# Attention in halves: value weights times g as f32r products of high and low parts, and raw expert weights in two places

## The reference

```python
h = h + attn(layernorm(h))   # q, k, v = x @ w_qkv, 16 heads of 64
                             # q = softmax(q * SCALE, axis=-1); k = softmax(k, axis=-2)
                             # context = q^T k over the tokens; out = context . v; out @ w_out + b_out
h = h + ffn(layernorm(h))    # sigmoid router, best 2 of 8 experts (4 of width 256, 4 of 512),
                             # relu(x @ w1)^2 @ w2, weighted by the two normalized probabilities
```

## Time and profile before

| | |
|---|---|
| median of 3 runs | 763.19 us (762.99 to 764.37) |
| the profiled execution | 760.92 us |
| its span | 759.1 us |
| TensorE matmul busy | 644.4 us (85%) |
| VectorE busy | 472.6 us (62%) |
| ScalarE busy | 304.7 us (40%) |
| GpSimd busy | 324.2 us (43%) |
| mean granted TensorE clock | 0.94 |

### The profile page before, as it was taken

How to read it: one execution, slowest core, us unless ns; L and a number is a source line. 1 busy time by engine, 2 the same in 40 slices (tenths; PEclk the granted TensorE clock), 3 DMA queues, 4 the chain that set the end, 5 groups by cost and what they waited for, 6 DMA issues and landing times. The chain is left out here.

```text
span 759.1 us, 15851 instructions
## 1 busy us (share of the span) xinstructions
PE 644.4 (85%) x5026; PEld 554.9 (73%) x5026; DVE 472.6 (62%) x1226; ACT 304.7 (40%) x664; POOL 324.2 (43%) x300
## 2 busy tenths in 40 slices
PE   6299677999999999999999998620999999988882
PEld 5299555788787877878878786510899999988772
DVE  2167566677987779777797775372645454555441
ACT  1324014445344353443534425302555555565551
POOL 6450134131370814608155170624144444466674
PEclk9699978999999999999999999955899999999997
DMA  7640288001110111101110020233244544467674
GB/s 235 206 92 2 56 214 306 3 1 56 44 70 2 57 56 55 59 8 69 39 57 29 11 75 1 82 116 108 60 80 72 86 81 78 81 102 116 106 116 49
DMA packets 38496, 59.44 MB, mean 78 GB/s; under 512 B 6110, under 2 KB 32218, under 8 KB 37786
## 3 DMA queue, kind: packets, MB, share of 16 engines
q1 hardware_dynamic: 23090, 35.76, 16.3%
q0 software_dynamic: 14496, 20.79, 15.0%
q10 hardware_dynamic: 808, 1.56, 0.7%
HBM read 29.22 MB, written 27.82 MB: 75 GB/s over the span
## 5 line engine op out<-in xcount | busy, mean ns | idle before, releaser
L1510 POOL DMA_INDIRECT out<-y,token_at x72 | 113.5, 1576 | 108.6 <-SPq L1490 107.4
L767 POOL DMA_INDIRECT queue_d<-row,slot x64 | 64.3, 1004 | 166.0 <-DVE slot L1079 129.2
L1589 DVE SCALAR_TENSOR_TENSOR act_w<-relu,queue_rows 128x512 f32<-128x512 f32 (+1 forms) x72 | 45.1, 627 | 99.0 <-ACT relu L1534 38.1
L1243 PE MATMUL bank<-xt_hi,w_first 128*128 128x512 f32 x256 | 94.9, 417 | 0.9 <-DVE second_half L957 0.9
L1243 PE MATMUL bank<-w_first,xt_hi 128*128 128x512 f32 x256 | 83.5, 408 | 2.2 <-DVE xt_lo L947 1.5
L759 POOL TENSOR_TENSOR second_half<-second_half,q_inv 128x512 f32<-128x512 f32 x64 | 64.9, 1042 | 43.1 <-DVE q_inv L966 43.0
L817 ACT ACTIVATE second_half<-second_half 128x512 f32<-128x512 f32 x64 | 39.6, 632 | 87.4 <-DVE second_half L957 77.1
L825 ACT ACTIVATE k_exps<-bank,k_negmax 128x512 f32<-128x512 f32 x64 | 44.1, 691 | 74.9 <-DVE k_negmax L973 74.8
L1631 PE MATMUL bank<-w_hi,a_hi 128*128 x220 | 67.7, 308 | 1.2 <-DVE a_lo L1595 0.9
L1631 PE MATMUL bank<-w_lo,a_hi 128*128 x220 | 61.5, 279 | 0.0
L1631 PE MATMUL bank<-w_hi,a_lo 128*128 x220 | 61.2, 278 | 0.0
(11 more groups left out here) (183 smaller groups left out, 1587.3 us busy)
## 6 DMA issues: line engine op xcount, KB each, us to landing
queue_rows<-queue_d SPq DMA_DIRECT2D x74, 129.0 KB
store<-in_L_ffn_w SPq DMA_DIRECT2D x4, 1536.0 KB, 9.2
out<-res SPq DMA_DIRECT2D x8, 512.0 KB, 2.9
h_d<-store SPq DMA_DIRECT2D x6, 512.0 KB, 9.0
h_in<-h_d SPq DMA_DIRECT2D x6, 512.0 KB, 4.0
wqk<-in_L_attn_w_qkv SPq DMA_DIRECT2D x1, 2048.0 KB, 8.6
queue_d<-filler SPq DMA_DIRECT2D x1, 1290.0 KB
out<-y,token_at POOLq DMA_INDIRECT x72
```

What stands on the lines that cost most here:

```text
L767: pool.indirect_dma_start(out=queue_d, in_=row[:, t, c, :], in_offset=None, out_offset=bass.IndirectOffsetOnAxis(ap=slot[:, TT * c + t:TT ...
L1243: last = nc.tensor.matmul(o, a, c, start=(n == 1), stop=(n == 3 * len(pairs)))
L1510: pool.indirect_dma_start(out=out, in_=y[:, j % RING, :], in_offset=None, compute_op=ALU.add, out_offset=bass.IndirectOffsetOnAxis(ap=toke ...
L1589: nc.vector.scalar_tensor_tensor(out=act_w[:, u % 2, 0:width], in0=relu[:, u % 2, 0:width], scalar=rows[:, u, DIM:DIM + 1], in1=relu[:, u ...
```

## The change

- `m_of` becomes `m_of(b, 0)` and `m_of(b, 1)`. Each takes four of the eight pairs of heads, for both 128-row parts of the result, as three f32r products: wv_hi x g_hi, wv_hi x g_lo, wv_lo x g_hi. All 48 add up in one PSUM bank.
- `g` (8 pairs) becomes `g_hi` and `g_lo` of 4 pairs, used once for each half. ScalarE's `g_take` becomes `g_high`, and VectorE gets `g_low`. `g_high` 2 and 3 wait for the first half of `m_of` (`g_used`).
- `wv_t` is split once, in step 0 (`wv_high`, `wv_low`). `wv_lo` lies where `wv_t` was.
- h of the convolution stays in a three-place `h_store`. The same memory later holds a two-place `store` and `wv_hi`. Pieces 0 and 1 are loaded at L661; piece 2 waits for `w1_low(0)` and piece 3 for `w1_low(1)`.
- On TensorE the first half of `m_of` stands behind q 6 and ahead of `g_of(1)`, and q 7 behind that. On VectorE `m_low` moves behind `k_max(b, 1)`, and `w1_low(0)` behind `g_low(3)`. On ScalarE `g_high` 2 and 3 stand behind `q_exps(b, 6)`.

```diff
@@ tower
-        store = sbuf(top, "store", [P, 3, TOTAL_W])
+        with ExitStack() as early:
+            h_store = sbuf(early, "h_store", [P, 3, TOTAL_W])
+        store = sbuf(top, "store", [P, 2, TOTAL_W])
+        wv_hi = sbuf(top, "wv_hi", [P, PAIRS, DIM], F32R)
+        sbuf(top, "unused", [P, TOTAL_W - PAIRS * DIM])
...
@@ sync
-                    for n in range(3):
+                    for n in range(KC):
                         sp.dma_start(raw_place(store, n), raw_piece((w1, w2), n)).then_inc(raw_in[n], 16)
...
-            sp.wait_ge(w1_lo_ready, 1)
-            sp.dma_start(raw_place(store, 3), raw_piece((w1, w2), 3)).then_inc(raw_in[3], 16)
+            for n in range(KC):
+                sp.wait_ge(w1_lo_ready, n + 1)
+                sp.dma_start(raw_place(store, KC + n), raw_piece((w1, w2), KC + n)).then_inc(raw_in[KC + n], 16)
@@ scalar
-            def g_take(b, n):
-                copy(g[:, 4 * (n // 2) + n % 2:4 * (n // 2) + 4:2], tail_bank(2 + n)[:].rearrange("p (a n) -> p a n", a=2),
-                     [(tail_psum, b.nth(TAIL_USES, 3 + n))], g_ready)
+            def g_high(b, n):
+                if n < 2:
+                    if not b.is_first(1):
+                        act.wait_ge(tail_psum, b.nth(TAIL_USES, 7 - TAIL_USES))
+                else:
+                    act.wait_ge(g_used, b.nth(1, 1))
+                copy(g_half(n), tail_bank(2 + n)[:].rearrange("p (a n) -> p a n", a=2),
+                     [(tail_psum, b.nth(TAIL_USES, 3 + n))], g_hi_ready)
...
+            def wv_high(b):
+                if b.is_first(1):
+                    act.wait_ge(h_stored, 16 * (BATCHES - 2))
+                    for par in range(2):
+                        act.wait_ge(loaded[par], 16)
+                    nc.scalar.activation(wv_hi[:], wv_t[:], ACT.Copy).then_inc(wv_hi_ready, 1)
@@ scalar step
                 q_exps(b, 2)
-                g_take(prev, 0)
-                g_take(prev, 1)
-                g_take(prev, 2)
-                g_take(prev, 3)
+                g_high(prev, 0)
+                g_high(prev, 1)
                 q_exps(b, 3)
                 q_exps(b, 4)
                 q_exps(b, 5)
                 q_exps(b, 6)
+                g_high(prev, 2)
+                g_high(prev, 3)
                 if b is None:
 
                     w1_high(prev, 0)
                     w1_high(prev, 1)
                 q_exps(b, 7)
                 k_exp(b, 0)
+                wv_high(b)
                 m_high(prev)
@@ vector
+            def g_low(b, n):
+                dve.wait_ge(g_hi_ready, b.nth(4, n + 1))
+                nc.vector.tensor_tensor(g_lo[:, n % 2:4:2], tail_bank(2 + n)[:].rearrange("p (a n) -> p a n", a=2),
+                                        g_hi[:, n % 2:4:2].bitcast(F32), ALU.subtract).then_inc(g_lo_ready, 1)
...
+            def wv_low(b):
+                if b.is_first(1):
+                    dve.wait_ge(wv_hi_ready, 1)
+                    nc.vector.tensor_tensor(wv_lo[:], wv_t[:], wv_hi[:].bitcast(F32), ALU.subtract).then_inc(wv_lo_ready, 1)
@@ vector step
                 route_slots(old)
-                if b is None:
-                    w1_low(prev, 0)
                 q_shift(b, 3)
                 q_total(b, 2)
                 q_shift(b, 4)
                 q_total(b, 3)
                 q_shift(b, 5)
                 q_total(b, 4)
+                g_low(prev, 0)
+                g_low(prev, 1)
                 q_shift(b, 6)
                 q_total(b, 5)
                 q_shift(b, 7)
                 q_total(b, 6)
+                g_low(prev, 2)
+                g_low(prev, 3)
+                if b is None:
+                    w1_low(prev, 0)
                 q_total(b, 7)
                 k_max(b, 0)
                 ln_stats(nxt)
+                k_max(b, 1)
+                wv_low(b)
                 m_low(prev)
-                k_max(b, 1)
                 add_attention(prev)
@@ tensor
-            def m_of(b):
-                pe.wait_ge(g_ready, b.nth(4, 4))
-                tail_free(b, 6)
+            def m_of(b, n):
+                pe.wait_ge(g_lo_ready, b.nth(4, 2 * n + 2))
+                if n == 0:
+                    tail_free(b, 6)
+                    if first(b):
+                        pe.wait_ge(wv_lo_ready, 1)
                 for kk in range(KC):
-                    for a in range(PAIRS):
-                        last = nc.tensor.matmul(tail_bank(6)[:, DIM * kk:DIM * kk + DIM],
-                                                wv_t[:, a, P * kk:P * kk + P], g[:, a],
-                                                start=(a == 0), stop=(a == PAIRS - 1))
-                last.then_inc(tail_psum, 1)
+                    o = tail_bank(6)[:, DIM * kk:DIM * kk + DIM]
+                    for a in range(4):
+                        w = slice(P * kk, P * kk + P)
+                        for x, (vw, gw) in enumerate(((wv_hi, g_hi), (wv_hi, g_lo), (wv_lo, g_hi))):
+                            last = nc.tensor.matmul(o, vw[:, 4 * n + a, w], gw[:, a],
+                                                    start=(n == 0 and kk == 0 and a == 0 and x == 0),
+                                                    stop=(n == 1 and kk == KC - 1 and a == 3 and x == 2))
+                last.then_inc(tail_psum if n else g_used, 1)
@@ tensor step
                 q_unit(b, 4)
                 g_of(prev, 0)
-                g_of(prev, 1)
                 q_unit(b, 5)
                 q_unit(b, 6)
+                m_of(prev, 0)
+                g_of(prev, 1)
                 q_unit(b, 7)
                 k_unit(b, 0)
-                m_of(prev)
+                m_of(prev, 1)
                 k_unit(b, 1)
```

More of the change, by code:

```diff
@@ L184, in tower @@
         with ExitStack() as attn_ctx:
-            wv_t = sbuf(attn_ctx, "wv_t", [P, PAIRS, DIM])
+            with ExitStack() as early:
+                wv_t = sbuf(early, "wv_t", [P, PAIRS, DIM])
+            wv_lo = sbuf(attn_ctx, "wv_lo", [P, PAIRS, DIM], F32R)
             wo = sbuf(attn_ctx, "wo", [P, PAIRS, DIM])
@@ L191, in tower @@
                 convolve(nc, conv_ctx, sem, bank, ident, x, embeddings, conv_w, conv_b, w_qkv, w_out, b_out,
-                         taps_d, store, h_in, loaded, router_w, rw_t, second_half, wqk_hi, wqk_lo, wv_t, wo, bo_all)
+                         taps_d, h_store, h_in, loaded, router_w, rw_t, second_half, wqk_hi, wqk_lo, wv_t, wo, bo_all)
             with ExitStack() as ctx:
-                attend(nc, ctx, sem, bank, ident, base, base0, rw_t, w1, w2, h_d, store, h_in, loaded, h_stored, raw_in,
-                       table, queue_d, out, second_half, wqk_hi, wqk_lo, wv_t, wo, bo_all,
+                attend(nc, ctx, sem, bank, ident, base, base0, rw_t, w1, w2, h_d, h_store, store, h_in, loaded, h_stored, raw_in,
+                       wv_hi, wv_lo, table, queue_d, out, second_half, wqk_hi, wqk_lo, wv_t, wo, bo_all,
                        w1_parts, w1_hi_ready, w1_lo_ready, w1_zero)
@@ L507, in raw_place @@
 def raw_place(store, n):
-    return store[:, n % 3] if n < KC else store[:, n % 3].rearrange("p (c n) -> p c n", n=DIM)
+    return store[:, n % 2] if n < KC else store[:, n % 2].rearrange("p (c n) -> p c n", n=DIM)
 def stored_h(store, b):
@@ L522, in piece @@
 def piece(store, n, dst):
-    r = store[:, n % 3]
+    r = store[:, n % 2]
     if n < KC:
@@ L536, in piece, with attend @@
     return [(r, dst[:, 4:WIDE * FC])]
-def attend(nc, ctx, sem, bank, ident, base, base0, rw_t, w1, w2, h_d, store, h_in, loaded, h_stored, raw_in,
-           table, queue_d, out, second_half, wqk_hi, wqk_lo, wv_t, wo, bo_all,
+def attend(nc, ctx, sem, bank, ident, base, base0, rw_t, w1, w2, h_d, h_store, store, h_in, loaded, h_stored, raw_in,
+           wv_hi, wv_lo, table, queue_d, out, second_half, wqk_hi, wqk_lo, wv_t, wo, bo_all,
            w1_parts, w1_hi_ready, w1_lo_ready, w1_zero):
@@ L558, in attend @@
     context = sbuf("context", [P, PAIRS, DH])
-    g = sbuf("g", [P, PAIRS, DIM])
+    g_hi = sbuf("g_hi", [P, PAIRS // 2, DIM], F32R)
+    g_lo = sbuf("g_lo", [P, PAIRS // 2, DIM], F32R)
     m_hi = sbuf("m_hi", [P, KC, DIM], F32R)
@@ L602, in attend @@
         sem(n) for n in ("k_exp_ready", "k_psum", "k_ready", "tail_chain", "tail_psum"))
-    ctx_ready, g_ready, m_hi_ready, m_lo_ready, res_added = (
-        sem(n) for n in ("ctx_ready", "g_ready", "m_hi_ready", "m_lo_ready", "res_added"))
+    ctx_ready, g_hi_ready, g_lo_ready, m_hi_ready, m_lo_ready, res_added = (
+        sem(n) for n in ("ctx_ready", "g_hi_ready", "g_lo_ready", "m_hi_ready", "m_lo_ready", "res_added"))
+    wv_hi_ready, wv_lo_ready, g_used = (sem(n) for n in ("wv_hi_ready", "wv_lo_ready", "g_used"))
     stats2_ready, var2_ready, rstd2_ready, row_ready, x2t_ready = (
@@ L647, in load @@
                         for later in range(2, BATCHES):
-                            store_h(sp, h_d, store, later).then_inc(h_stored, 16)
```

(15 more changed lines are left out.)

2 lines of the change are left out of this document (added).

## The result

The changed kernel takes 820.51 us (median of 4 runs, 818.43 to 824.26), the kernel before 763.09 beside it: ratio 1.077, 95% interval 1.072 to 1.082. The forecast was 825 in a range of 800 to 848. The profiled execution took 818.43 us, against 760.92, which is 57.5 us more where the sum had 61.3. Ratios leave out slow executions; there was one, of 1611.87 us beside three near 752, in g1_first.

A forecast was written before the change was run, and what follows sets the result against it. The attention stage was taken to run at the pace of TensorE's own list. Walk 43.5, clock 15.4, last step 2.2 and weight split 0.2 sum to 61.3 us over 760.92, about 825 as a median, range 800 to 848.

The forecast's parts named there:

- The walk of the step: Attention stage's inner step: TensorE waits 4.8, 2.25 and 1.2 us; net loss 6.45 us, 38.6 us over steps 2 to 7.
- the products: m_of on TensorE: 48 f32r matmuls take 5.8 us instead of 6.72, saving 0.9 us a step.
- the old wait: TensorE's 0.91 us wait ahead of g_of(1) in the kernel before, counted as 0.9 us saved per step.
- Step 1: First attention step with VectorE further ahead: TensorE stands 3.3 us first, and the step loses 4.9 us.
- The clock: TensorE's clock falls at the first pause of each of seven steps, 2.2 us each, 15.4 us in all.
- short pauses do nothing: Amid long groups of work, no clock fall was forecast behind a pause as short as the second, 2.25 us.
- Rival (b): The clock falls at the second pause as well: up to 37.8 us instead of 15.4, total 835 to 848; chance 0.22.
- Rival (a): The pauses come but TensorE's clock holds: 809 us; chance 0.2.
- The last step: w1_high moves behind g_high(3) on ScalarE, ahead of m_high, so m_high starts later: +2.2 us, ends 0.5 and 4.
- Step 0: One-time split of the value weights (wv_high on ScalarE, wv_low behind k_max 1): +0.2 us, ends 0 and 2.5.
- the raw pieces: Later loads of raw expert weights on SP's queue: nothing, up to 1.5 us if their writes collide.

The follow-up runs named there:

- g1_first: all_early2 with g_of(1) ahead of the first half of m_of on TensorE: 752.17 us, ratio 1.012 to the kernel before, on chip B.
- fill_all: The changed kernel with all three TensorE waits of steps 2 to 7 filled with unread f32r matmuls: 793.06 against 742.81 us, ratio 1.067, chip B.
- all_early2: The changed kernel with g_low, g_high 2 and 3 and m_low moved earlier on VectorE and ScalarE, TensorE's list unchanged: 784.55 us, ratio 1.029, chip A.
- filled_wait2: The changed kernel with 18 unread f32r matmuls ahead of the first half of m_of in steps 2 to 7: 821.65 us, ratio 1.078, chip A.
- places_alone: The kernel before with only the two-place store and the later loads of raw pieces 2 and 3: 742.82 against 742.81 us, chip B.
- enqueue_late: all_early2 with GpSimd's eight indirect DMAs issued behind q_norm 7 in steps with a current batch: 779.85 us, ratio 1.049, chip B.
- low_early2: The changed kernel with g_low 0 and 1 right behind shift 3 on VectorE instead of behind total 4: 816.54 us, ratio 1.072, chip A.
- m_low_first2: The changed kernel with m_low ahead of k_max 1 on VectorE, as before the change: 818.92 us, ratio 1.076, chip A.
- no_waits: g1_first with m_high ahead of k_exp 0, m_low behind k_max 0, last step's w1_high 1 behind m_high: 792.60 against 759.74 us, ratio 1.041, chip C.

## Why the prediction was right, by its own steps

**The walk of the step: right.** It put the three waits at 4.8, 2.25 and 1.2 us; they are 4.63, 2.13 and 0.99. With -0.9 for the products (two halves of 2.9 us, as measured in g1_first: 328.40 to 331.32 and 334.53 to 337.45) and -0.9 for the old wait the step was to lose 6.45. fill_all, which holds full clock, gives 6.4. The points between agree too: counted from the start of `g_of(0)`, the walk has the first half at 8.7, the second at 17.7 and `attention_of` at 23.7 us, and in fill_all they start at 8.7, 17.9 and 23.7 (302.46, 311.62 and 317.50, less 293.76). all_early2 and g1_first show the cause: TensorE's products are the same, and 36 us on chip A and nearly all of the loss on chip B go away by order alone.

**Step 1: right,** 4.9 forecast for the walk, 4.86 measured (waits of 3.05, 2.13 and 0.99).

**The clock: right in kind, too large.** It falls once in each of steps 2 to 7, as forecast, but a fall costs 1.5 us, not 2.2, and in step 1, behind 3.05 us, it doesn't fall: some 9 us in place of 15.4. That it held there is no rule, since the same step lost its clock twice in filled_wait2. The mis-sized term is the 2.2 us. It was the mean of two prices, 2.7 and 1.7; the lower one belongs to a stretch of the length that came. The forecast that short pauses do nothing also failed, in filled_wait2. Rival (b) had that, and in the inner steps of the changed kernel itself it didn't come. Rival (a), a clock that holds, left out these 9 us. By the Trainium skill, "TensorE: Matmul & The Clock Gate", section "HAM oscillation — how this bites in real kernels", a wait in each turn of a loop can throttle TensorE again in every turn; this trace agrees in six of the seven steps.

**The last step: too small.** 2.2 forecast, 5.1 measured. The step named `w1_high` ahead of `m_high`; that came, but later than thought:

```profile
526.06 1.09 ACT L816 ACTIVATE g_hi<-bank 128x512 fp32r<-128x512 f32 x2 [7.26 <-PE bank L1346]
535.98 1.09 ACT L816 ACTIVATE g_hi<-bank 128x512 fp32r<-128x512 f32 x2 [8.83 <-remote]
536.95 2.85 ACT L889 ACTIVATE w_first<-store 128x1024 fp32r<-128x1024 f32 x2
539.70 2.86 ACT L889 ACTIVATE w_second<-store 128x1024 fp32r<-128x1024 f32 x2
543.13 0.60 ACT L816 ACTIVATE m_hi<-bank 128x512 fp32r<-128x512 f32 x1 [0.57 <-PE bank L1364]
```

`g_of(1)` ran from 532.64 to 533.73, and the copy that waits for it started 2.2 us behind that: the late signal once, on the path. The clock was at half from 528.9 to 532.3 and from 535.7 to 542.5, too, against one stretch of 3.4 us in the last step before. How the 5.1 us part between the order, the signal and the clock no run shows.

**The rest: right.** Step 0 and the way into step 1 cost 0.7 us (0.2 forecast), the experts' stage 0.1, and places_alone has the raw pieces at nothing. The sum, forecast and measured: step 1 with its clock 7.1 and 4.9, steps 2 to 7 51.9 and 46.8, last step 2.2 and 5.1, the rest 0.2 and 0.8; 61.3 and 57.5 in the traces (the parts add to 57.6 by rounding). The clock's share was too large by some 6 us and the last step's too small by 3; that these errors point opposite ways is luck, and the total looks closer for it than its parts.

**What stays open.** What makes TensorE's signals late. Shown: it comes behind the first half while GpSimd issues its eight indirect DMAs, on chips A and C, and the signals then come at or 1.5 us behind the end of the eighth; in step 1, where it issues none, the same kernels have prompt signals; on chip B g1_first has prompt signals in spite of them (at 284.25, amid DMAs from 277.99 to 287.94). That the DMAs hold the signals up is likely by this and not shown: the one run that moved them, enqueue_late, ran on chip B alone, and all_early2 was not run there. Open too is what the clock goes by. In the changed kernel, low_early2 and filled_wait2 its falls begin 54.61 us apart, once a step, and steps last 54.5 to 54.8 us in all three, though low_early2 has 0.9 us less of waiting in a step and pays it back with twice the stretch at half clock. What ties the step to the fall there no run shows. No version tried beats the kernel before.

## What to carry to other kernels

When a product moves ahead in an in-order engine's list, walk the list of the engine that feeds it, with durations of one traced step, up to the last operand: the wait is the difference, and here it was right to 0.25 us. Move the producers along with the consumer; that, with `g_of(1)` ahead of the first half, took nearly all of this loss back on one chip. Don't count a removed wait as won before the trace shows it: the clock and late signals took back most of it in low_early2, m_low_first2 and no_waits. Compare versions on one chip.

## What the runs showed of the hardware

- The same waits of 3.05 and 2.1 us in step 1 left TensorE's clock at 2.4 GHz in the changed kernel and in fill_all, and brought it to 1.2 GHz twice in filled_wait2 and m_low_first2, for 3.4 us each. In g1_first it fell behind waits of some 0.65 and 0.99 us in two steps of six and held behind equal ones in others; with every wait at 0.57 us or less it held throughout (fill_all). The length of a pause alone doesn't tell it.
- A fall of 3.4 us amid matmuls cost 1.5 us (25.21 less 22.13 for two in step 1; 54.61 less 53.12; 48.74 less 47.28 in g1_first).
- TensorE's signals around the first half of `m_of` (that of the half itself in no_waits, of `g_of(1)` elsewhere) reached other engines 3.6 to 4.6 us (chip A, steps 2 to 6) and 4.5 to 6.1 us (chip C) behind the last matmul of their group while GpSimd issued eight indirect DMAs, most of them at the end of the eighth or 1.5 us behind it; on chip B g1_first, with the same list on TensorE as no_waits, had it after 0.3 us.
- The same two kernels differ in ratio by chip: all_early2's was 1.029 on one and 1.050 on another, with intervals of 0.006 or less on either side.
